# A two-layer perceiver on one core: scores in groups of 32 rows, queries taken straight from PSUM, fillers at two places

## What is computed

```python
x = x + L0_xattn(norm(x), ctx)       # q = x@Wq, k = ctx@Wk, v = ctx@Wv, 8 heads of 64, softmax, @Wo + bo
x = x + L0_attn(norm(x))             # 16 heads of 16, causal: att[j > i] = -inf; softmax; @Wo
x = x + L0_ffn(norm(x))              # router (top 2 of 16 experts), shared and routed MLPs of width 352
x = x + L1_xattn(norm(x), ctx, ctx)  # q = x@Wq + bq, k = ctx@Wk + bk, v = ctx@Wv + bv, 16 heads of 16
x = x + L1_attn(norm(x))             # linear attention with elu, then a gelu feed-forward of width 1024
x = x + L1_ffn(norm(x))              # each of 8 experts takes its 32 best rows: softmax(x@Wr), top_k, gelu MLP + b1, b2
```

## Time and profile before

| what | value |
|---|---|
| median of 3 runs | 1137.12 us (1134.63 to 1140.26) |
| profiled execution, its own time | 1140.25 us |
| its span | 1138.1 us |
| mean granted TensorE clock | 0.987 |
| PE busy | 1107.5 us, 97% of the span |
| DVE, ACT, POOL busy | 57%, 59%, 20% |
| PE on the chain that ended last | 85% of the span |

### The profile page before, as it was taken

The page is one execution under the profiler, slowest core; times in us unless marked ns, Lnnn a source line. Parts: engine busy times, 40 slices in busy tenths (PEclk is TensorE's granted clock), DMA queues, the critical chain, the costliest instruction groups (busy, mean ns, idle before and its releaser), DMA issues.

```text
span 1138.1 us, 28418 instructions
## 1 busy us (share of the span) xinstructions
PE 1107.5 (97%) x9890; PEld 917.1 (81%) x9890; DVE 645.3 (57%) x1091; ACT 668.3 (59%) x1107; POOL 222.8 (20%) x317
## 2 busy tenths in 40 slices
PE   6999899999999999999999999999998999999998
PEld 4788688888888888888875888888887888888874
DVE  4999654444444444444454788888886434444342
ACT  1889433433434334343332688888888999999631
POOL 0000100000000000000103777777770110000120
PEclk8999899999999999999999999999999999999989
DMA  3444531110000100001174576667666897555290
GB/s 133 129 138 141 218 152 28 28 34 30 28 28 28 37 28 28 28 28 28 45 298 158 188 231 227 223 228 228 224 221 199 303 313 241 189 194 194 94 403 8
DMA packets 63496, 162.15 MB, mean 142 GB/s; under 512 B 6896, under 2 KB 8368, under 8 KB 58160
## 3 DMA queue, kind: packets, MB, share of 16 engines
q1 hardware_dynamic: 54592, 119.06, 32.3%
q0 software_dynamic: 8880, 42.76, 9.9%
HBM read 122.96 MB, written 38.80 MB: 142 GB/s over the span
## 4 chain that ended last, share of the span: by engine, by line
PE 85%; DVE 6%; issue 5%; DMA 2%; ACT 1%; DVEq 1%; POOL 0%; ACTq 0%; SPq 0%
PE ps L732 55%; PE ps L916 8%; PE ps L982 8%; PE ps L767 2%; PE ps L720 2%; DVE wide L1500 1%; DMA q_le<-k_mem 1%; DVE wide L1508 1%; PE ps L778 1%; PE ps L782 1%; PE ps L779 1%; PE ps L780 1%; PE ps L781 1%; PE ps L1318 1%; DMA ring<-ex_in 1%
## 5 line engine op out<-in xcount | busy, mean ns | idle before, releaser
L1572 DVE TENSOR_TENSOR wide<-wide,probs 128x1024 f32<-128x1024 f32 x97 | 118.8, 1225 | 225.2 <-ACT probs L568 224.8
L1500 DVE TENSOR_TENSOR wide<-ps,wide 128x512 f32<-128x512 f32 (+1 forms) x194 | 184.9, 953 | 28.3 <-PE ps L732 23.8
L553 ACT CAST wide<-ps 128x512 bf16<-128x512 f32 x294 | 162.1, 586 | 32.3 <-PE ps L732 27.1
L568 ACT ACTIVATE probs<-ps 128x512 f32<-128x512 f32 x196 | 114.7, 599 | 81.0 <-PE ps L732 81.0
L732 PE MATMUL ps<-q_ha,t_ha 128*128 128x512 f32 x392 | 157.6, 402 | 4.3 <-DVE q_le L1427 3.8
L578 ACT ACTIVATE probs<-ps 128x1024 f32<-128x1024 f32 x132 | 128.0, 1026 | 18.5 <-PE ps L732 16.5
L1508 DVE TENSOR_TENSOR wide<-wide 128x512 bf16<-128x512 bf16 (+1 forms) x194 | 107.3, 553 | 13.6 <-ACT wide L553 3.1
L732 PE MATMUL ps<-q_ab,q_hk 128*128 128x512 f32 x392 | 107.4, 395 | 1.3 <-DVE q_ab L1433 1.3
L732 PEld LDWEIGHTS ps<-q_ha,t_ha 128*128 128x128 f32 x392 | 75.7, 193 | 22.8 <-DVE q_le L1427 4.3
L563 ACT COPY weights_q<-ps 128x512 f32<-128x512 f32 x48 | 28.1, 586 | 106.0 <-PE ps L916 90.0
L435 POOL DMA_DIRECT2D tiles_q<-ex_in x1 | 0.5, 527 | 431.9 <-PE ps L916 431.9
(11 more groups left out here) (421 smaller groups left out, 2388.6 us busy)
## 6 DMA issues: line engine op xcount, KB each, us to landing
raw<-ctx_in SPq DMA_DIRECT2D x147, 256.0 KB, 2.7
k_mem<-q_hk SPq DMA_DIRECT2D x49, 512.0 KB, 3.0
v_mem<-probs SPq DMA_DIRECT2D x49, 256.0 KB, 3.4
wide<-v_mem SPq DMA_DIRECT2D x49, 256.0 KB, 4.0
q_le<-k_mem SPq DMA_DIRECT2D x17, 512.0 KB, 4.3
q_ab<-k_mem SPq DMA_DIRECT2D x16, 512.0 KB, 4.0
q_hk<-k_mem SPq DMA_DIRECT2D x16, 512.0 KB, 4.1
ring<-ex_in POOLq DMA_DIRECT2D x5, 1088.0 KB, 13.0
```

Of the source, the lines that this page charges most:

```text
L553: act.copy(half16[:, c:c + 512], ps[:, back_bank(layer, q) + u, :]).then_inc(sem(f"half{layer}"), 1)
L568: act.activation(e_keep[GT * slot + j][:, u * 512:(u + 1) * 512], ps[:, s_bank[j][u], :], ACT.Exp).then_inc(sem("exp0"), 1)
L1500: dve.tensor_tensor(r, scores, r, ALU.max).then_inc(sem(f"front{layer}"), 1)
L1572: dve.tensor_tensor(run[:, 0:1024], run[:, 0:1024], e, ALU.add).then_inc(sem("lsum"), 1)
```

## The change

It edits five places.

1. **Folding.** The scale goes into the mask, so DVE spreads straight from PSUM, without `qt`, and signals each of the four parts. Three fillers go ahead of the folding matmuls and seven behind them. ACT takes `q_ha` and `q_he` (`keep_queries0`), between its first and its second `round_hi`; DVE keeps `q_b`, `q_la` and `q_le`. The DMA of `wa` is cut: the part for `wk` first, the rest (1152 of its 1794 KB) after the first two context groups.
2. **Self attention.** Keys are spread over two halves of each 32 rows (twice 128x256, from PSUM). Scores are eight matmuls of 32 rows by 256 columns, four row groups into four banks. The mask goes in first, 14 fillers are gone, the maximum is subtracted by a further matmul per bank (`minus` by `top`), and the exponential is one instruction per bank. Five fillers become three. Heads stand in another order, and the rows of `Wo` with them.
3. **Queries of layer 1.** The bias is put into banks 4 and 5 by four 128x128 matmuls ahead of the eight fillers; DVE spreads straight from PSUM; ACT makes `qt` (`keep_queries1`), for the store to memory alone.
4. **Last router.** `bias1` 0 and 1 are each followed by four fillers; four fillers follow the router; `bias1` 2 and 3, with two fillers each, take the place of the ten.
5. **Semaphores.** The last experts' weights count on the semaphores of layer 0's places.

```diff
@@ sync
-            sp.dma_start(wa[:, wk0:XQ0W], xq0_in[:, wk0:XQ0W]).then_inc(sem("xq0_loaded"), 16)
+            wv0 = XQ0["wva"]
+            sp.dma_start(wa[:, wk0:wv0], xq0_in[:, wk0:wv0]).then_inc(sem("wk0_loaded"), 16)
+            def load_first(g, slot, first):
+                load(0, g, slot, first)
+                if first and slot == 1:
+                    sp.dma_start(wa[:, wv0:XQ0W], xq0_in[:, wv0:XQ0W]).then_inc(sem("xq0_loaded"), 16)
@@ scalar
+            def keep_queries0():
+                for c in range(2):
+                    act.wait_ge(sem("q_folded"), c + 1)
+                    cs = slice(c * 512, (c + 1) * 512)
+                    act.copy(q_ha[:, cs], ps[:, 1 + 3 * c, :]).then_inc(sem("q_high"), 1)
+                    act.copy(q_he[0:CB + 1, cs], ps[0:CB + 1, 3 + 3 * c, :]).then_inc(sem("q_high"), 1)
+            def keep_queries1():
+                for b in range(2):
+                    act.wait_ge(sem("q_diag"), 4 + 1 + b)
+                    act.mul(qt[0:CB, b * 256:(b + 1) * 256], ps[0:CB, 4 + b, 0:256], float(HD[1]) ** -0.5)\
+                        .then_inc(sem("q_kept"), 1)
...
-                act.wait_ge(sem("logit_a"), c + 1)
-                for h in range(4 * c, 4 * c + 4):
-                    last = act.activation(run[:, h * P:(h + 1) * P], ps[:, 2 + c, (h % 4) * P:(h % 4 + 1) * P], ACT.Exp,
-                                          bias=sm[:, h:h + 1])
-                last.then_inc(sem("prob_a"), 1)
+                act.wait_ge(sem("shift_a"), c + 1)
+                act.activation(run[:, c * 512:(c + 1) * 512], ps[:, 2 + c, :], ACT.Exp).then_inc(sem("prob_a"), 1)
@@ tensor, fold
-                pe.wait_ge(sem("q_diag"), 1)
-                pe.wait_ge(sem("xq0_loaded"), 16)
+                keep_warm(3, 7)
+                pe.wait_ge(sem("wk0_loaded"), 16)
                 for c in range(2):
+                    pe.wait_ge(sem("q_diag"), 2 * c + 2)
...
+                keep_warm(7, 7)
                 pe.wait_ge(sem("q_chunk"), 2)
@@ tensor, cross(1)
                     keys1(0, 0, True)
+                    query_bias()
                 turn_x(3 * layer, 3 * layer, xn, fill=(0, 8)[layer])
+            def query_bias():
+                pe.wait_ge(sem("xq1_loaded"), 16)
+                for u in range(UNITS):
+                    bq = wx1[:, XQ1["bq"] + u:XQ1["bq"] + u + 1].to_broadcast([P, P])
+                    pe.matmul(ps[:, 4 + u // 2, u % 2 * P:(u % 2 + 1) * P], ident, bq, start=(u % 2 == 0), stop=False,
+                              skip_group_check=True)
@@ tensor, self attention
-            keep_warm(14)
+            for c in range(4):
+                pe.matmul(ps[:, 2 + c, :].rearrange("p (h n) -> p h n", n=P), minus[:],
+                          future[:].unsqueeze(1).to_broadcast([P, 4, P]), start=True, stop=False, skip_group_check=True)
             pe.wait_ge(sem("q_a"), 1)
+            for b in range(2):
+                pe.wait_ge(sem("k_diag"), b + 1)
+                for r in range(4):
+                    rs = slice(32 * r, 32 * r + 32)
+                    last = pe.matmul(ps[:, 2 + r, b * 256:(b + 1) * 256], qt[rs, b * P:(b + 1) * P],
+                                     probs[rs, b * 256:(b + 1) * 256], start=False, stop=False, skip_group_check=True)
+                    if b == 1:
+                        last.then_inc(sem("s_a"), 1)
             for c in range(4):
-                pe.wait_ge(sem("k_diag"), c // 2 + 1)
-                mm(ps[:, 2 + c, :], qt[:, (c // 2) * P:(c // 2 + 1) * P], probs[:, c * 512:(c + 1) * 512], 0, 2)
-                mm(ps[:, 2 + c, :].rearrange("p (h n) -> p h n", n=P), minus[:],
-                   future[:].unsqueeze(1).to_broadcast([P, 4, P]), 1, 2).then_inc(sem("s_a"), 1)
-            keep_warm(5, 7)
+                pe.wait_ge(sem("logit_a"), c + 1)
+                pe.matmul(ps[:, 2 + c, :].rearrange("p (h n) -> p h n", n=P), minus[:],
+                          top[:, 4 * c:4 * c + 4].unsqueeze(2).to_broadcast([P, 4, P]), start=False, stop=True,
+                          skip_group_check=True).then_inc(sem("shift_a"), 1)
+            keep_warm(3, 7)
@@ tensor, last router
-            for i in range(3):
+            for i in range(2):
                 bias1(i)
+                keep_warm(4, 4)
             turn_x(7, 6, xn, fill=0, bank=4)
...
-            bias1(3)
+            keep_warm(4, 4)
             pe.wait_ge(sem("scores_r"), 1)
             pe.transpose(ps[0:E1, 6, 128:256], sm[:, 32:32 + E1], ident).then_inc(sem("scores_t"), 1)
-            keep_warm(10, 5)
+            for i in range(2, 4):
+                bias1(i)
+                keep_warm(2, 4)
             pe.wait_ge(sem("picked"), 1)
@@ vector, fold
-                link(dve.tensor_scalar(qt[:], ps[:, 0, :], float(HD[0]) ** -0.5, None, ALU.mult))
                 for b in range(4):
-                    last = dve.tensor_tensor(
+                    dve.tensor_tensor(
                         scr[:, b * 2 * P:(b + 1) * 2 * P].rearrange("p (h q) -> p h q", h=2),
-                        qt[:, b * P:(b + 1) * P].unsqueeze(1).to_broadcast([P, 2, P]),
-                        spread(cst[:, CONST["mask2"]:CONST["mask2"] + 2], P), ALU.mult)
-                last.then_inc(sem("q_diag"), 1)
+                        ps[:, 0, b * P:(b + 1) * P].unsqueeze(1).to_broadcast([P, 2, P]),
+                        spread(cst[:, CONST["mask2"]:CONST["mask2"] + 2], P), ALU.mult).then_inc(sem("q_diag"), 1)
...
-                    dve.tensor_copy(q_ha[:, cs], ps[:, b, :])
                     dve.tensor_copy(q_b[:, cs], ps[:, b + 1, :])
-                    link(dve.tensor_copy(q_he[0:CB + 1, cs], ps[0:CB + 1, b + 2, :]))
+                    dve.wait_ge(sem("q_high"), 2 * c + 1)
@@ vector, self attention
-            link(dve.tensor_copy(qt[:, D:2 * D], ps[:, 0, 0:D]))
             for b in range(2):
-                dve.tensor_tensor(probs[:, b * 1024:(b + 1) * 1024].rearrange("p (h q) -> p h q", h=8),
-                                  qt[:, D + b * P:D + (b + 1) * P].unsqueeze(1).to_broadcast([P, 8, P]),
-                                  spread(cst[:, CONST["mask8"]:CONST["mask8"] + 8], P), ALU.mult).then_inc(sem("k_diag"), 1)
+                dve.tensor_tensor(probs[:, b * 256:(b + 1) * 256].rearrange("p (s q) -> p s q", s=2),
+                                  ps[:, 0, b * P:(b + 1) * P].unsqueeze(1).to_broadcast([P, 2, P]),
+                                  spread(cst[:, CONST["half"]:CONST["half"] + 2], P), ALU.mult).then_inc(sem("k_diag"), 1)
```

More of the change, by code:

```diff
@@ L83 @@
 CONST["side"] = 464 + TOPK
-CONSTW = 464 + TOPK + 2
+CONST["half"] = 464 + TOPK + 2
+CONSTW = 464 + TOPK + 4
 LA = {"wq": 0, "wk": 512, "wv": 1024, "wo": 1536}
@@ L341, in ones_row @@
                 sp.dma_start(kp[slot][ONE, :].bitcast(F32), kp[0][ONE, :].bitcast(F32)).then_inc(sem(f"k_in{slot}"), 16)
-            groups(sp, lambda g, slot, first: load(0, g, slot, first))
+            def load_first(g, slot, first):
+                load(0, g, slot, first)
+                if first and slot == 1:
+                    sp.dma_start(wa[:, wv0:XQ0W], xq0_in[:, wv0:XQ0W]).then_inc(sem("xq0_loaded"), 16)
+            groups(sp, load_first)
             sp.wait_ge(sem("hi0"), GROUPS)
@@ L759, in queries1 @@
                         c = XQ1["wq"] + k * 512 + u * P
-                        last = mm(ps[:, 4 + u // 2, u % 2 * P:(u % 2 + 1) * P], wx1[:, c:c + P], xt[:, k * P:(k + 1) * P], k, DK)
+                        last = pe.matmul(ps[:, 4 + u // 2, u % 2 * P:(u % 2 + 1) * P], wx1[:, c:c + P],
+                                         xt[:, k * P:(k + 1) * P], start=False, stop=(k == DK - 1), skip_group_check=True)
                     if u % 2 == 1:
@@ L824, in scores1 @@
                         fresh = first and t < depth
+                        if layer == 1 and first and t == 1:
+                            pe.wait_ge(sem("q_kept"), 2)
                         for n in range(2 * units):
```

53 lines of the change are left out of this document (30 added, 23 removed).

## The result

Over four runs each, the changed kernel took 1124.66 us in the median (1124.24 to 1127.05), the kernel before 1136.53 (1134.63 to 1140.26): a ratio of 0.9883, interval 0.9863 to 0.9903, 11.9 us less. The profiled execution of the changed kernel took 1124.4 us, with a span of 1122.6.

What follows compares the result with a forecast made beforehand. PE, with 85% of the chain, was taken as the bound, through its waits, fillers and low clock. Terms -5.1 - 3.3 - 2.5 - 0.6 - 2.2 = -13.7 gave 1126.5 (profiled) or 1123.4 (median); forecast 1125, range 1120 to 1131 us.

Steps and rivals of the forecast that it cites:

- Folding, start (-5.1): At the folding: the first pass starts at 17.95 us instead of 23.05, 5.1 us less.
- Clock in the first pass (-3.3): First pass of layer 0: at full clock the first four tiles take 3.74 us instead of 7.04, 3.3 less.
- the rival that the pass doesn't gain what its start gains: First pass: late loads or a low clock lose 3.3 and some of 5.1 us, giving 1130; chance 0.07.
- The reason that I gave, fillers and short stands: Folding: fillers and PE standing only some 0.8 us in all keep the clock at 1.00.
- Self attention (-2.5): Layer 0's self attention: 2.5 us less, taken between -2.9 and a case with the clock falling, costing about 1.2 more.
- my row of the column groups: Self attention: experts' matmuls in four column groups, used to take eight 32-row matmuls as two rounds of 0.43 us.
- the rival's mechanism: Self attention: the clock falls, or row groups run one after another, 1.2 us more each; both give 1127; chance 0.12.
- Queries (-0.6): Layer 1's queries: PE waits for nothing and the second pair of scores starts at 633.85, not 634.43, 0.6 less.
- Last router (-2.2): Last router: choice at 1108.8 instead of 1111.65 us (-2.85), some 0.6 back from an earlier clock fall; 2.2 less.
- the prediction's own sign: Prediction wrong if the first pass waits for loads, or the clock falls at a thinned place and stays low afterwards.
- The rival of thin fillers: Last router: fillers too thin, the clock falls among `bias1`, +1.75 instead of -2.2 us, time 1129; chance 0.19.
- The middle between the profiled execution and the median: Whole kernel: 1125 us, taken between 1126.5 from the profiled execution and 1123.4 from the median.

Runs made afterwards that it cites:

- fold_conversions_dve: Changed kernel with all ten folded-query conversions on DVE and PE starting behind all four spreads, the ten fillers kept: 1127.37 us, ratio 0.9918.
- self_as_before: Changed kernel with layer 0's self attention (scores, spread, subtraction, fillers, layout of heads) put back as before: 1127.32 us, ratio 0.9907.
- fold_no_fillers: Changed kernel without the three and the seven fillers at the folding: 1125.24 us, ratio 0.9889.
- second_pass_paced: second_pass_fillers with POOL loading `wx` first and alone, then `wlb` and the five experts' loads one by one behind passing tiles: 1120.90 us, ratio 0.985.
- fold_as_before: Changed kernel with ten conversions on DVE, PE starting behind all four spreads, and the folding's ten fillers out: 1129.88 us, ratio 0.9931.
- router_as_before: Changed kernel with the last router's fillers and bias matmuls put back as before: 1124.41 us, ratio 0.9887.
- router_denser: Changed kernel, last router: third `bias1` replaces four fillers behind the router's matmuls, five fillers follow the fourth, three follow the turnings: 1123.68 us, ratio 0.9869.
- router_full_depth: router_as_before with the four 16-row `bias1` replaced by 128-row matmuls of the same width, output not the reference's: 1121.52 us, ratio 0.9841.
- second_pass_fillers: Changed kernel with 12 more fillers in front of layer 0's second pass: 1124.23 us, ratio 0.9887.
- three_places_paced: second_pass_paced plus router_denser's edits and four instead of eight fillers at layer 1's queries: 1119.41 us, ratio 0.9835.

## Why the prediction was right, and where it was wrong

**Folding, start (-5.1).** Measured -4.6. The spread from PSUM took 0.36 a piece (0.43 taken), and the matmuls 5.33 us for both halves. The last half's conversions took 1.93 us, as in the sum (1.9). What was late is what stands ahead of them: PE started the folding at 11.16, not 10.8, and its 24 matmuls took 5.33 and not 5.16. So the last conversion ended at 18.43 and not 17.95.

**Clock in the first pass (-3.3).** Measured -3.8, of which 0.5 is before's one wait in the pass, so -3.3 by the clock, which was at 1.00 from 5 to 116 us. There was no wait for loads: in the changed kernel the rival that the pass doesn't gain what its start gains is out. Its mechanism exists: in two variants, fold_conversions_dve and self_as_before, a context load came late once, and PE waited 0.7 us. The reason that I gave, fillers and short stands, holds with both parts: 1.7 us from the stands and 1.6 from the fillers, by fold_no_fillers and one execution each.

**Self attention (-2.5).** Measured -2.8. The row groups ran four at once (1.16 us for eight; 0.86 calculated, 3.4 as the bound). The Trainium skill ("TensorE: Matmul & The Clock Gate", Part 3, Packing small matmuls) gave 1.1 us by its speedup of 3.07, and the trace agrees with it better than with my row of the column groups. The clock did not fall in the changed kernel's trace (1.00 from 560 to 585), but it did in two other traces with the same self attention (0.50 from 567.8 to 571.2 in second_pass_paced, and from 576.2 to 579.6 in fold_as_before), where the sixteen turnings took 2.85 and 2.57 us instead of 1.91. So the rival's mechanism exists and comes in some executions. It fell 1.5 and 2.0 us ahead of the first turning, so the turnings did not bring it, and no run here shows whether they count for the clock.

**Queries (-0.6).** Measured -0.8. PE waited for no spread.

**Last router (-2.2): this step failed.** It gave +0.3. Two terms of it failed, by about as much. Up to the choice it is -1.6 and not -2.85: from the `bias1` to the choice it takes 11.0 us, 12.6 before. The sum had two `bias1` and four fillers take 2.6 us beside DVE's search, with the search setting the choice. They took 3.9, each `bias1` some 1.05 and not 0.87, and PE came 0.9 us behind DVE. About 0.5 of that is the clock's fall ahead of the choice; where it held (10.5 us in four traces of this order) PE still set the choice. The other term is that the clock would fall a little earlier than now, some 0.6 back. The low stretch moved onto the gathering, which before ran at full clock, and gave 1.9 back. By the prediction's own sign, a clock that falls there and stays low into the experts, this part was wrong. The starts in PE's timeline of all the traces:

| Order at the last router | traces | first `bias1` to choice | to experts' first matmul |
|---|---|---|---|
| three `bias1`, then one (before, router_as_before) | 2 | 12.7, 12.1 | 16.4, 15.9 |
| changed kernel's | 8 | 10.5 to 11.8 | 16.0 to 16.8 |
| router_denser's | 3 | 10.5, 10.2, 11.4 | 16.4, 13.9, 17.4 |
| full depth | 1 | 10.0 | 14.9 |

The changed kernel's order brings the choice forward each time, and loses it again behind it each time. The rival of thin fillers had the right mechanism, but far too much of it ahead of the choice: it had the last two `bias1` at 2.0 us each, which would have made 1129. In the changed kernel's trace the fall came 9.8 us behind the first `bias1`.

**The sum.** -13.7 forecast, -11.7 measured at the edited places. The middle between the profiled execution and the median, 1125, came out within 0.4 us by luck: the missing 2.0 and the 1.6 by which the middle lay above the median-based 1123.4 cancelled. The mechanism holds for four of the five parts.

**What stays open.** What decides at the last router between 13.9 and 17.4 us with the same instructions. The depth of the matmuls seems to count (router_full_depth), and the order alone doesn't settle it. That it hangs on the moment at which the chip looks at PE is argued and not shown; the Trainium skill (same page, Part 1, What's actually happening) says that the point of transition varies from run to run of one kernel. It says so of the rise at a kernel's start; the three traces show such a spread for the fall.

## What to carry to other kernels

A place where the clock is low can hide a wait: when the clock is mended, look for what lands next, here a weights' load with 8.6 us of a waiting DVE behind it, and mend both together. When fillers or thin matmuls are moved, follow the low stretch to where it goes; it pays only if it lands on a wait and not on real matmuls. Take the sum at the edited places, not the difference of two spans: here 3.9 of 15.5 us were in code that nobody had touched. And compare lengths of a stage, not the times at which it ends: in fold_no_fillers the second pass starts only 0.5 us late, since the first had started 1.1 early, and the stage itself was 1.6 longer.

## What the runs showed of the hardware

Layer 1's first pass has two paces with the same code. Groups of POOL's instructions from 640 to 850 us, first of the changed kernel, then of router_denser (count, busy us, mean ns, idle before):

```profile
L462 POOL TENSOR_TENSOR t_la<-raw,t_ha 128x256 fp32r<-128x256 f32 x42 | 49.3, 1175 | 3.3
L465 POOL TENSOR_TENSOR t_b<-raw,t_b 64x256 fp32r<-64x256 f32 x42 | 30.9, 735 | 3.3
L460 POOL TENSOR_TENSOR t_b<-raw,ones 128x256 fp32r<-128x256 f32 x42 | 25.5, 607 | 0.0
```

```profile
L465 POOL TENSOR_TENSOR t_b<-raw,t_b 64x256 fp32r<-64x256 f32 x43 | 50.4, 1173 | 3.4
L460 POOL TENSOR_TENSOR t_b<-raw,ones 128x256 fp32r<-128x256 f32 x42 | 46.6, 1111 | 0.0
L462 POOL TENSOR_TENSOR t_la<-raw,t_ha 128x256 fp32r<-128x256 f32 x43 | 31.9, 741 | 3.4
```

The same five instructions take 3.73 us a group in the one and 4.24 in the other: one of them is stretched to 1.2 us in the first, two in the second. They are those that lie beside DVE's maximum of two tiles in bf16 (0.69 us; it takes 0.84 in the mean in router_denser, too). In the slow pace POOL waits for nothing but its own instructions, and PE's weight loads wait for its `t_b` 5.2 us in sum from 640 to 850 us; in the changed kernel POOL waits for PE there. From the bias of layer 1's queries to the first `bias1` of the last router it takes 474.6 to 477.4 us instead of 469.9 to 472.0. Three traces have the slow pace (second_pass_fillers, router_denser, three_places_paced), and those three executions lie 4.1, 6.6 and 6.7 us above their medians. So the pace makes a good part of the scatter of these three; the executions without a trace can't be told. The Trainium skill ("SBUF — State Buffer", Who interferes with whom) says that a DVE instruction with two inputs in SBUF and a GpSimd instruction that reads it lock each other out, and that the order of issue decides who waits; the two paces look like two such orders that keep themselves going, which no run here tested.

The granted clock and PE's stands, over all the traces: behind 2.4 us or more of standing it fell each time but one (0.50 after 2.41 and 3.81 us; held after 2.51 in second_pass_fillers at 136.5). Behind 2.32 it fell, behind 2.0 for a short time (fold_no_fillers), behind 2.25 and 1.67 it held (fold_conversions_dve, fold_as_before). One place shows it best, as nobody edited it: at the end of layer 1's first pass (842.3 us in the changed kernel) PE stands for 1.86 us in all fourteen traces, and the clock fell there to 0.50 for 3.4 us in six and held in eight. So the length of a stand tells the chance and not the outcome. In before's trace it fell behind matmuls of 16 rows with PE busy all through (0.50 from 1101.5, PE without a stand from 1098.9 to 1101.9).
